# A macaron block with two routed FFNs on one core: closer pacing of GpSimd's transfers, three gather buffers in rotation, and a mix placed by tables

## The chip, the cores and the metric

The kernel runs on one NeuronCore of a Trainium2 chip: TensorE (PE) for matmuls, VectorE (DVE), ScalarE (ACT), GpSimd (POOL) and SyncE (SP, which here only issues DMAs). The metric is the device time of one execution in microseconds; lower is better. Kernels are compared by the median of several runs.

## The reference

x has 8 batches of 512 tokens of 128 channels. Three residual layers follow each other:

```
x = x + 0.5 * moe(layernorm(x))          # 8 experts, top 2 of a softmax, F = 512
x = x + rwkv(layernorm(x))               # token shift, k, v, r, a scan over the sequence, output projection
x = x + 0.5 * moe(layernorm(x))          # the same weights again

moe:  probs = softmax(x @ gate); w, i = top_k(probs, 2); w = w / w.sum()
      out = sum over experts e of  (silu(x @ w1[e]) * (x @ w3[e])) @ w2[e] * w_e
rwkv: k = mix_k(x) @ Wk; v = mix_v(x) @ Wv; r = sigmoid(mix_r(x) @ Wr)
      a running, decayed, numerically shifted sum over the 512 positions of e^k * v and of e^k; r * ratio @ Wo
```

## The kernel before

Tokens are sorted by expert so that TensorE works on tiles of 128 rows that all belong to one expert. There are 177 such tiles. They are grouped in nine *runs* (0 to 8): runs 0 to 3 are the first FFN, each for two batches ("units" .0 and .1), 23 tiles each; runs 4 to 8 are the second FFN. Runs begin at tiles 0, 23, 46, 69, 92, 101, 131, 140 and 162. For each run:

- **Routing** (`NORM`, then `CHOOSE`): layernorm, gate logits, the two picks, counts per expert, and the slot of each token.
- **Scatter** (POOL, L694): for each unit four groups of 128 tokens, twice (top 2), so 8 indirect DMAs a unit, write token rows to their slots in DRAM (`rows_in`). SP then loads the tiles (`rin`), up to six loads ahead.
- **Tiles**: TensorE transposes a tile, multiplies by w1 and w3 (`pa`, `pb`), ACT makes the silu, DVE the product `h` (L1084), TensorE multiplies by w2 three tiles later (`py`), ACT copies `y` out and stores it in DRAM (`rows_out`).
- **Gather** (POOL, L708): 8 indirect DMAs a unit bring the rows of y back to their tokens, in a buffer `yg`. Then DVE's **combine** (L1094) adds them, weighted, to the residual `xres`, eight instructions a unit.
- After a combine of runs 0 to 3 comes the `MIX` chain of that unit (the rwkv layer): DVE, ACT and PE take turns in some twenty steps, from `mstats` to `add`. After a combine of runs 4 to 8 the unit is written to the output.

What is not tile work (routing, combines, mix) is laid between the tiles by a planner, `make_plan`, that runs when the kernel is built. It has a clock with a cost for each step, `ready()` (which steps could start) and `choose()` (the one due first that fits in the slack of a tile). The result is a list: behind tile t, engine by engine, these steps. Every engine runs its list strictly in order, so a step whose input isn't there yet holds all tiles behind it on its engine. The list of POOL's transfers is made by `send()`, which takes `SPACE` us for each.

POOL issues its 256 indirect DMAs in that order. The first 16 follow each other freely. The next 232 are paced, with two rules for each: wait until DVE has made the `h` of tile number `gate`, and wait until the memset behind the transfer before has ended (`s_pace`), then issue, then a small memset (L724). The last 8 (the gather of run 8) are free again. The gather buffer is chosen by unit number (`yg[:, b]`, two of them), so a gather of unit b waits until the last gather of any unit b has been combined. Gathers happen in this order: 0.0, 0.1, 1.0, 1.1, 2.0, 2.1, 3.0, 3.1, 4.0, 4.1, 5.0, 5.1, 6.0, 6.1, 7.0, 8.0.

## Time and profile before

| | us |
|---|---|
| median of 3 runs | 676.24 (674.56 to 677.45) |
| the profiled execution | 672.78 |
| its span, first to last instruction | 671.0 |
| mean granted TensorE clock | 0.946 of full |
| busy: PE, DVE, ACT, POOL | 528.1, 412.7, 319.7, 297.2 |

The profile is of one execution. An instruction's row gives its start, its length, its engine and line, and in brackets how long the engine had been idle before it and what ended that. Tiles can be counted in time by the DVE instruction that makes `h`, one for each tile.

### The profile page before, as it was taken

How to read it: one execution, taken by the hardware profiler on the slowest of the kernel's cores; microseconds unless marked ns; L12 is line 12 of the kernel's file. 1: busy time of each engine (PE TensorE's matmuls, PEld its weight loads, DVE VectorE, ACT ScalarE, POOL GpSimd, SP SyncE). 2: the span in 40 equal slices, each digit the busy share in tenths (PEclk: the TensorE clock that was granted, in tenths of full speed). 3: DMA queues.
4: the chain of work that ended last, by engine and by line, in shares of the span. 5: the costliest groups of instructions: out<-in, count | busy, mean ns of one | idle time of the engine just before them, and what ended most of it. 6: DMA issues, size and time to landing. Idle time of an engine off the chain costs nothing. (4 is left out here: it accounts for less than half of the span.)

```text
span 671.0 us, 18790 instructions
## 1 busy us (share of the span) xinstructions
PE 528.1 (79%) x5866; PEld 482.5 (72%) x5866; DVE 412.7 (62%) x1218; ACT 319.7 (48%) x703; POOL 297.2 (44%) x499
## 2 busy tenths in 40 slices
PE   2136899993899889898999859989789999989500
PEld 1125799893788878677888749878789899879500
DVE  4845975221678789588897848859786443333311
ACT  5433754441484566654656615854645344334100
POOL 1270356666540550565405655046005555525543
PEclk9999999998799999998999959999799999999955
DMA  8943234442221221222211133111112324322311
GB/s 287 325 143 99 84 112 147 136 134 67 76 77 41 64 72 49 73 64 63 78 49 45 53 99 83 44 60 49 57 34 77 100 81 127 85 64 72 86 52 43
DMA packets 89016, 59.57 MB, mean 89 GB/s; under 512 B 10208, under 2 KB 82656, under 8 KB 88928
## 3 DMA queue, kind: packets, MB, share of 16 engines
q1 hardware_dynamic: 55248, 29.97, 15.3%
q0 software_dynamic: 8192, 16.79, 8.9%
q10 hardware_dynamic: 25488, 11.61, 5.9%
q8 instruction: 58, 0.95, 0.6%
q14 instruction: 30, 0.25, 0.1%
HBM read 28.65 MB, written 29.69 MB: 87 GB/s over the span
## 5 line engine op out<-in xcount | busy, mean ns | idle before, releaser
L694 POOL DMA_INDIRECT rows_in<-parts,slot x128 | 132.5, 1035 | 232.9 <-DVE h L1084 136.4
L1084 DVE TENSOR_TENSOR h<-sil,pb 128x512 f32<-128x512 f32 x177 | 120.9, 686 | 145.8 <-PE pb L1201 59.3
L1215 PE MATMUL py<-ffn_w,h 128*128 x1416 | 199.0, 284 | 13.6 <-ACT yrow L753 12.4
L1215 PEld LDWEIGHTS py<-ffn_w,h 128*128 128x128 f32 x1416 | 175.3, 195 | 20.0 <-issue 13.9
L1201 PE MATMUL pa<-rT,ffn_w 128*128 128x128 f16 (+1 forms) x1752 | 152.7, 234 | 36.8 <-DVE h L1084 26.0
L708 POOL DMA_INDIRECT yg<-rows_out,slot x128 | 123.8, 968 | 130.3 <-issue 53.6
L1201 PEld LDWEIGHTS pa<-rT,ffn_w 128*128 x1752 | 124.9, 100 | 52.6 <-issue 41.1
L1201 PE MATMUL pb<-rT,ffn_w 128*128 128x128 f16 (+1 forms) x1752 | 157.1, 233 | 0.1
L1201 PEld LDWEIGHTS pb<-rT,ffn_w 128*128 x1752 | 124.4, 99 | 7.6 <-issue 0.3
L768 ACT ACTIVATE sil<-pa 128x512 f32<-128x512 f32 x177 | 105.4, 595 | 42.6 <-PE pa L1201 32.8
L748 ACT ACTIVATE rT<-pT 128x512 f16<-128x512 f16 (+1 forms) x112 | 56.8, 508 | 92.5 <-PE pT L1188 81.2
L753 ACT ACTIVATE yrow<-py 128x128 f32<-128x128 f32 x177 | 48.6, 274 | 90.0 <-PE py L1215 64.2
L1094 DVE SCALAR_TENSOR_TENSOR xres<-yg,wts,xres 128x128 f32<-128x128 f32 x128 | 36.5, 348 | 63.8 <-DMA yg<-rows_out,slot 63.3
L1188 PE MATMUL pT<-ident,rin 128*128 128x128 f16 x354 | 39.1, 224 | 13.0 <-DMA rin<-rows_in 13.0
L787 ACT ACTIVATE xn<-xres,shift,rstd 128x128 f32<-128x128 f32 x96 | 39.3, 486 | 9.1 <-issue 5.8
L724 POOL MEMSET pace<- 128x64 uint8 x232 | 39.1, 169 | 0.2
L1188 PEld LDWEIGHTS pT<-ident,rin 128*128 128x128 f16 x354 | 26.2, 100 | 14.4 <-DMA rin<-rows_in 13.2
L1268 PE MATMUL bkA<-ident,xn 128*128 128x128 f32 x64 | 12.2, 324 | 29.2 <-ACT xn L787 28.4
L1268 PEld LDWEIGHTS bkA<-ident,xn 128*128 128x128 f32 x64 | 8.8, 170 | 30.0 <-issue 28.8
L1253 PE MATMUL bkB<-xT,qkv_w 128*128 128x512 f16 x96 | 23.4, 379 | 3.4 <-ACT xT L817 3.4
L874 DVE BATCH_NORM_STATS2 stats<-xres 128x6 f32<-128x128 f32 x96 | 20.8, 279 | 4.2 <-DMA xres<-in_x 3.8
L904 DVE TENSOR_TENSOR parts<-xn,parts 128x512 f16<-128x512 f32 x24 | 16.5, 690 | 9.4 <-ACT parts L801 7.7
(155 smaller groups left out, 442.0 us busy)
## 6 DMA issues: line engine op xcount, KB each, us to landing
rows_out<-yrow ACTq DMA_DIRECT2D x177, 64.0 KB
rin<-rows_in SPq DMA_DIRECT2D x65, 128.0 KB
rows_in<-zrow SPq DMA_DIRECT2D x34, 128.0 KB
shared<-in_w SPq DMA_DIRECT2D x16, 256.0 KB, 7.0
rin<-rows_in SPq DMA_DIRECT2D x47, 64.0 KB
rows_in<-zrow SPq DMA_DIRECT2D x2, 1472.0 KB, 12.2
xres<-in_x SPq DMA_DIRECT2D x4, 512.0 KB, 5.7
ffn_w<-in_w SPq DMA_DIRECT2D x8, 256.0 KB
```

The lines of the kernel that those rows point to most:

```text
L694: pool.indirect_dma_start(rows_in[g][:], bass.IndirectOffsetOnAxis(ap=slot[:, c, at:at + 1], axis=0), parts[:, at, :], None).then_inc(s_sc ...
L708: pool.indirect_dma_start(yg[:, b, c, j, :], None, rows_out[SET[run]][0:PASS_STEPS[PASS[run]] * T, :], bass.IndirectOffsetOnAxis(ap=slot[: ...
L724: pool.memset(pace[:], 0).then_inc(s_pace, 1)
L748: act.activation(rT[:, q % 2, :, 0:n], pT[:, :, 0:n], ACT.Copy).then_inc(s_rT, 1)
L753: act.activation(yrow[:, t % YSLOTS, :], py[:], ACT.Copy).then_inc(s_yrow, 1)
L768: act.activation(sil[:, t % 2, :], pa[t % 2][:], ACT.Silu, scale=1.0 / WS).then_inc(s_sil, 1)
L787: ins = act.activation(xn[:, at, j, :], xres[:, js, :][:, j, :], ACT.Identity, bias=shift[:, u, j:j + 1], scale=rstd[:, u, j:j + 1])
L1084: dve.tensor_tensor(h[:, t % RING, :], sil[:, t % 2, :], pb[t % 2][:], ALU.mult).then_inc(s_h, 1)
L1094: ins = dve.scalar_tensor_tensor(xj, yg[:, b, c, j, :], wts[:, c, u * JU + j:u * JU + j + 1], xj, ALU.mult, ALU.add)
L1188: mm = pe.transpose(pT[:, part, n * T:(n + 1) * T], rin[:, q % SLOTS, n, part * D:(part + 1) * D], ident16[:])
L1201: mm = pe.matmul(bank[:, i * cols:(i + 1) * cols], weight_bytes[:, bass.ds(experts[expert_of(t)] * 4 + at, 2 * P)].bitcast(F16), rT[:, q % ...
L1215: mm = pe.matmul(py[:], h[:, step % RING, at:at + T], w, start=(c == 0), stop=(c == FC - 1))
```

## The change

- The pacing memset grows from 64 to 192 bytes a partition and gets four buffers. It now waits for the memset four transfers back, and the DMA itself waits for none. The wait for DVE's tile number is gone: the gate is still in the list, and is not used.
- The gather buffers become three, taken in the order of the gathers, whatever the unit. A gather waits for the combine of the gather three before it. The planner (`in_use`) knows this.
- The last gather (8.0) has a semaphore for each group of 128 tokens (`s_last`). Its combine goes group by group (`combine_last`), and SP writes the output in four parts.
- The planner's costs change a little (`SPACE` 1.6 to 1.5, `LAND` 4.0 to 4.5, others), and two tables are added: `NOT_BEFORE` holds a step back until a tile number, `DUE_SHIFT` makes four chains due later. All 449 steps and 232 paced transfers are the same ones; their order is new.

```diff
+GSLOTS = 3
-PACE = 64
+PACE = 192
+PACES = 4
...
-HOP, LAND, SEND, LOAD = 0.1, 4.0, 1.1, 3.0
-SLIP = {"dve": 6.0, "act": 3.1, "pe": 2.0}
-SPACE = 1.6
+HOP, LAND, SEND, LOAD = 0.1, 4.5, 1.1, 3.0
+SLIP = {"dve": 6.3, "act": 2.9, "pe": 2.0}
+SPACE = 1.5
+DUE_SHIFT = {
+    "stats5.0": 12, "stats2.0": 110, "pick1.0": 173, "combine3.1": 179
+}
+NOT_BEFORE = {
...
+    "place21.0": 8, "hi2.0": 10, "hi3.0": 11, "scatter1.0": 12, "lo2.0": 14, "count2.0": 20, "turn3.1": 20,
...
+        self.due = (due[0] + DUE_SHIFT.get(f'{steps[0]}{run}.{unit}', 0),) + due[1:]
...
-        if any(t is None for t in times):
+        if any(t is None for t in times) or tile < NOT_BEFORE.get(f'{step}{c.run}.{c.unit}', EARLY):
...
+    def in_use(run, unit):
+
+        order = [p[2:] for p in plan if p[1] == "gather"]
+        n = order.index((run, unit))
+        return n >= GSLOTS and "combine" not in gathered[order[n - GSLOTS]].ends
...
-        yg = sb("yg", [P, UG, TOPK, JU, D])
+        yg = sb("yg", [P, GSLOTS, TOPK, JU, D])
...
+                    if (run, b) == GATHERS[-1]:
+                        for j in range(JU):
+                            sp.wait_ge(s_lastc, j + 1)
+                            sp.dma_start(ov[:, js, :][:, j, :], xres[:, js, :][:, j, :]).then_inc(s_out, 16)
+                        return
...
-                if (j, c) == (0, 0):
-                    before = [p[1:] for p in PLAN if p[1] == "gather" and p[3] == b]
-                    at_b = before.index(("gather", run, b))
-                    if at_b:
-                        pool.wait_ge(s_comb, count(("combine",), ("combine", before[at_b - 1][1], b)))
+                n = GATHERS.index((run, b))
+                if (j, c) == (0, 0) and n >= GSLOTS:
+                    pool.wait_ge(s_comb, count(("combine",), ("combine", *GATHERS[n - GSLOTS])))
...
-            for sent, (gate, name, *one) in enumerate(TRANSFERS):
-                wait(pool, s_h, gate)
-                wait(pool, s_pace, sent)
+            for sent, (_, name, *one) in enumerate(TRANSFERS):
                 if name == "scatter":
                     scatter(*one)
                 else:
                     gather(*one)
-                pool.memset(pace[:], 0).then_inc(s_pace, 1)
+                wait(pool, s_pace, sent - PACES + 1)
+                pool.memset(pace[:, sent % PACES, :], 0).then_inc(s_pace, 1)
...
+            def combine_last(run, b):
+
+                u, js = units(run, b)
+                slot_ = (len(GATHERS) - 1) % GSLOTS
+                for j in range(JU):
+                    xj = xres[:, js, :][:, j, :]
+                    dve.wait_ge(s_last[j], 16 * TOPK)
+                    for c in range(TOPK):
+                        ins = dve.scalar_tensor_tensor(xj, yg[:, slot_, c, j, :],
+                                                       wts[:, c, u * JU + j:u * JU + j + 1], xj, ALU.mult, ALU.add)
+                        if c == 0:
+                            link(ins)
+                    ins.then_inc(s_lastc, 1)
```

Two places show how the rows move. The first is on POOL, where its first gather (unit 0.0) begins. `rows_in2` and `rows_in3` are written by scatters of runs 2 and 3, `yg` by gathers. Before:

```order
L694 DMA rows_in3<-parts,slot 2944x256 [waits transfer_spaced,h_made]
L724 MEMSET pace 128x64
L708 DMA yg<-rows_out0,slot 128x128 [waits y_stored4,y_stored5,y_stored3,y_stored6,y_stored2,y_stored7,y_stored1,y_stored8,y_stored0,y_stored9,transfer_spaced,h_made]
L724 MEMSET pace 128x64
L708 DMA yg<-rows_out0,slot 128x128 [waits transfer_spaced,h_made]
```

And after:

```order
L727 DMA rows_in2<-parts,slot 2944x256
L755 MEMSET pace 128x192 [waits transfer_spaced]
L739 DMA yg<-rows_out0,slot 128x128 [waits y_stored5,y_stored6,y_stored4,y_stored7,y_stored3,y_stored8,y_stored2,y_stored9,y_stored1,y_stored0]
L755 MEMSET pace 128x192 [waits transfer_spaced]
L739 DMA yg<-rows_out0,slot 128x128
```

Before, 39 paced transfers stand ahead of this gather (runs 1 and 2 complete, and 7 of run 3). After, 26 do: run 1 and ten of run 2; the other six of run 2 and all of run 3 stand behind the gathers of 0.0 and 0.1. The combine of 0.0 stands behind 35 `h` on DVE before, and behind 37 after.

The second place is the end of DVE's list: the combines of 7.0 and of 8.0. Before, both use buffer 0:

```order
L1094 SCALAR_TENSOR_TENSOR xres<-yg,wts,xres 128x128 [waits gathered1]
L1094 SCALAR_TENSOR_TENSOR xres<-yg,wts,xres 128x128 x3
L1094 SCALAR_TENSOR_TENSOR xres<-yg,wts,xres 128x128 [waits dve_chain]
L1094 SCALAR_TENSOR_TENSOR xres<-yg,wts,xres 128x128 x3
L1094 SCALAR_TENSOR_TENSOR xres<-yg,wts,xres 128x128 [waits gathered0,combined]
```

And after:

```order
L1125 SCALAR_TENSOR_TENSOR xres<-yg,wts,xres 128x128 [waits gathered2,combined]
L1125 SCALAR_TENSOR_TENSOR xres<-yg,wts,xres 128x128 x3
L1125 SCALAR_TENSOR_TENSOR xres<-yg,wts,xres 128x128 [waits dve_chain]
L1125 SCALAR_TENSOR_TENSOR xres<-yg,wts,xres 128x128 x3
L1140 SCALAR_TENSOR_TENSOR xres<-yg,wts,xres 128x128 [waits last_gathered0,combined]
L1140 SCALAR_TENSOR_TENSOR xres<-yg,wts,xres 128x128 [waits dve_chain]
L1140 SCALAR_TENSOR_TENSOR xres<-yg,wts,xres 128x128 [waits last_gathered1]
```

Unit 7.0 has moved to buffer 2, and of the last unit only two instructions now stand behind the last group's arrival.

## Rows read from the trace of the kernel before

**Rows 1.** The page: granted TensorE clock in 40 slices, and two groups.

```profile
PEclk9999999998799999998999959999799999999955
...
L708 POOL DMA_INDIRECT yg<-rows_out,slot x128 | 123.8, 968 | 130.3 <-issue 53.6
...
L724 POOL MEMSET pace<- 128x64 uint8 x232 | 39.1, 169 | 0.2
```

**Rows 2.** Instructions on `h` by stretch: PE, PEld, DVE busy (DVE's count is tiles).

```profile
57.50:151.50 94.00, 34.22 (x254) 30.77 (x255) 23.33 (x34) 1.00 0.39 115
151.50:240.70 89.20, 26.78 (x192) 23.92 (x191) 15.60 (x23) 0.92 0.23 64
240.70:400.50 159.80, 49.21 (x346) 43.47 (x344) 30.14 (x44) 0.95 0.23 65
400.50:501.70 101.20, 34.22 (x241) 29.77 (x240) 20.54 (x30) 0.97 0.19 54
501.70:599.00 97.30, 38.55 (x278) 33.59 (x279) 23.01 (x34) 1.00 0.32 90
```

**Rows 3.** What DVE waited for, gathers only: whole span, 150:240, 600:627, 627:671.

```profile
DVE xres L1094 <- DMA yg<-rows_out,slot: 63.3, 14, 13.1
...
DVE xres L1094 <- DMA yg<-rows_out,slot: 18.0, 3, 13.1
...
DVE xres L1094 <- DMA yg<-rows_out,slot: 0.3, 1, 0.3
...
DVE xres L1094 <- DMA yg<-rows_out,slot: 32.1, 3, 12.7
```

**Rows 4.** Timeline of DVE: the combine of unit 0.0.

```profile
165.39 2.32 DVE L1094 SCALAR_TENSOR_TENSOR xres<-yg,wts,xres 128x128 f32<-128x128 f32 x8 [13.12 <-DMA yg<-rows_out,slot]
```

**Rows 5.** Timeline of PE after that wait.

```profile
169.98 1.46 PE L1201 MATMUL pa<-rT,ffn_w 128*128 128x128 f16 x12 [13.49 <-DVE h L1084]
```

**Rows 6.** Busy by engine (PE, PEld, DVE, ACT, POOL), then granted clock.

```profile
169.00:175.10 6.10, 5.12 (x40) 5.06 (x41) 4.11 (x15) 3.10 (x8) 3.83 (x8) 0.51 0.21 58
```

**Rows 7.** Timeline of POOL: a scatter of run 3, and the first gather.

```profile
136.41 0.97 POOL L694 DMA_INDIRECT rows_in<-parts,slot  x1 [0.75 <-issue]
...
149.67 0.99 POOL L708 DMA_INDIRECT yg<-rows_out,slot  x1 [0.79 <-DVE h L1084]
```

**Rows 8.** Timeline of PE at the start of run 5.

```profile
388.65 0.61 PE L1188 MATMUL pT<-ident,rin 128*128 128x128 f16 x4 [4.08 <-DMA rin<-rows_in]
...
397.60 1.46 PE L1201 MATMUL pa<-rT,ffn_w 128*128 128x128 f16 x12 [5.25 <-issue]
```

**Rows 9.** Timeline of POOL in the tail, units 6.0 to 8.0.

```profile
601.76 0.95 POOL L708 DMA_INDIRECT yg<-rows_out,slot  x1 [9.90 <-DVE h L1084]
...
646.06 0.95 POOL L708 DMA_INDIRECT yg<-rows_out,slot  x1 [0.75 <-POOL pace L724]
...
651.79 0.95 POOL L708 DMA_INDIRECT yg<-rows_out,slot  x1 [4.61 <-DVE xres L1094]
653.05 0.95 POOL L708 DMA_INDIRECT yg<-rows_out,slot  x1 [0.30 <-issue]
...
660.55 0.94 POOL L708 DMA_INDIRECT yg<-rows_out,slot  x1 [0.30 <-issue]
```

**Rows 10.** Timeline from 661 to the end: the last combine and write.

```profile
663.28 2.31 DVE L1094 SCALAR_TENSOR_TENSOR xres<-yg,wts,xres 128x128 f32<-128x128 f32 x8 [12.26 <-DMA yg<-rows_out,slot]
665.68 0.37 SPq L651 DMA_DIRECT2D out<-xres  x1
```

**Rows 11.** Timeline of ACT: the last y copied out and stored.

```profile
631.65 0.28 ACT L753 ACTIVATE yrow<-py 128x128 f32<-128x128 f32 x1 [1.29 <-issue]
```

**Rows 12.** Timeline of POOL: a memset at the start, a scatter at 35 us.

```profile
0.73 0.20 POOL L671 MEMSET ident<- 128x128 f32 x1 [0.29 <-POOLq L1344]
...
35.38 1.96 POOL L694 DMA_INDIRECT rows_in<-parts,slot  x1 [0.30 <-issue]
```

**Rows 13.** Busy by engine (PE, PEld, DVE, ACT, POOL) in two stretches.

```profile
400.50:501.70 101.20, 91.97 (x1149) 85.60 (x1148) 83.30 (x242) 58.19 (x124) 29.99 (x52) 0.97 0.19 54
501.70:599.00 97.30, 90.52 (x1144) 86.53 (x1145) 42.80 (x125) 40.80 (x94) 53.07 (x94) 1.00 0.32 90
```

More of the change, by code:

```diff
@@ L157, in __init__ @@
     def __init__(self, steps, run, unit, due, start, follows=()):
-        self.steps, self.run, self.unit, self.due, self.start = steps, run, unit, due, start
+        self.steps, self.run, self.unit, self.start = steps, run, unit, start
+        self.due = (due[0] + DUE_SHIFT.get(f'{steps[0]}{run}.{unit}', 0),) + due[1:]
         self.follows, self.ends = list(follows), {}
@@ L187, in tile @@
         q, half, _ = TILE_OF[t]
-        up1 = max(self.free["pe"], self.rT[q] + HOP, self.h.get(t - 2, 0.0) + HOP) + UP
+        up = UP if paired(t) else UP_ALONE
+        up1 = max(self.free["pe"], self.rT[q] + HOP, self.h.get(t - 2, 0.0) + HOP) + up
         if t > SKEW:
@@ L191, in tile @@
         turned = self.turn(q + 1, up1) if t + 1 < TILES and TILE_OF[t + 1][1] == 0 else up1
[L192 removed]
+        up3 = turned + up
         silu = max(self.free["act"], up1 + HOP) + SILU
@@ L311, in ask @@
         waiting.append([due, at, name, run, [(b, j, c) for b in units for j in range(JU) for c in range(TOPK)]])
+    def in_use(run, unit):
+        order = [p[2:] for p in plan if p[1] == "gather"]
+        n = order.index((run, unit))
+        return n >= GSLOTS and "combine" not in gathered[order[n - GSLOTS]].ends
     def send(tile, until):
         while True:
-            now = [w for w in waiting if w[1] <= until and not (w[2] == "gather" and any(
-                c.next() == "combine" for c in chains if c.unit == w[4][0][0] and gathered.get((c.run, c.unit)) is c
-                and c.run < w[3]))]
+            now = [w for w in waiting if w[1] <= until and not (w[2] == "gather" and in_use(w[3], w[4][0][0]))]
             at = max([free["pool"]] + [min((w[1] for w in now), default=until)])
@@ L385, in count @@
     return order.index(upto) + 1
+GATHERS = [p[2:] for p in PLAN if p[1] == "gather"]
 def run_of(t):
@@ L445, in macaron_kernel @@
         zrow = sb("zrow", [P, 2 * D], F16)
-        pace = sb("pace", [P, PACE], U8)
+        pace = sb("pace", [P, PACES, PACE], U8)
         e_desc = sb("e_desc", [P, JG, E])
@@ L558, in macaron_kernel @@
         s_yst = [sem(f"y_stored{i}") for i in range(YSLOTS)]
-        s_gat = [sem(f"gathered{b}") for b in range(UG)]
+        s_gat = [sem(f"gathered{i}") for i in range(GSLOTS)]
+        s_last = [sem(f"last_gathered{j}") for j in range(JU)]
+        s_lastc = sem("last_combined")
         s_comb = sem("combined")
@@ L665, in _ @@
             last_steps(step)
-            sp.wait_ge(s_out, 16 * B)
+            sp.wait_ge(s_out, 16 * (B - 1 + JU))
         @block.gpsimd
@@ L702, in gather @@
                         pool.wait_ge(s_yst[k], 16 * len(range(k, PEND[run], YSLOTS)))
[L703 to L707 removed]
+                n = GATHERS.index((run, b))
+                if (j, c) == (0, 0) and n >= GSLOTS:
+                    pool.wait_ge(s_comb, count(("combine",), ("combine", *GATHERS[n - GSLOTS])))
                 pool.indirect_dma_start(
[L709 to L710 removed]
+                    yg[:, n % GSLOTS, c, j, :], None, rows_out[SET[run]][0:PASS_STEPS[PASS[run]] * T, :],
+                    bass.IndirectOffsetOnAxis(ap=slot[:, c, at:at + 1], axis=0)).then_inc(
+                        s_last[j] if n + 1 == len(GATHERS) else s_gat[n % GSLOTS], 16)
             def every(run, units):
@@ L1088, in combine @@
                 u, js = units(run, b)
-                runs = [p[2] for p in PLAN if p[1] == "gather" and p[3] == b]
-                dve.wait_ge(s_gat[b], 16 * TOPK * JU * (runs.index(run) + 1))
+                n = GATHERS.index((run, b))
+                dve.wait_ge(s_gat[n % GSLOTS], 16 * TOPK * JU * (n // GSLOTS + 1))
                 for c in range(TOPK):
@@ L1106, in step @@
                 if name == "combine":
-                    combine(run, b)
+                    (combine_last if (run, b) == GATHERS[-1] else combine)(run, b)
                 if name in ("stats", "mstats"):
```

10 lines of the change are left out of this document (4 added, 6 removed), and 7 rows, old and new, of the table NOT_BEFORE.

## The prediction

> **What bounds the kernel now.** I read the page first, for the slices in which the clock or PE's digit falls; then the instructions on `h` by stretch, since one of DVE's is one tile; then what DVE and PE waited for; and last the timelines of POOL, DVE and PE at the longest of those waits. The reader is to see three things.
>
> First, in most stretches the tiles go at a steady pace that all three compute engines set together: 44 tiles in 159.8 us (3.63 each), 30 in 101.2 (3.37), 34 in 97.3 (2.86) [rows 2]. PE is busy 92.0 of 101.2 us there, DVE 83.3 [rows 13]. Nothing in the change makes this work smaller, so the gain must come from waits.
>
> Second, one stretch is slow without more work: 23 tiles in 89.2 us, 3.88 each, at a mean clock of 0.92 [rows 2]. DVE stands 13.12 us before the combine of unit 0.0, because the gather has not landed [rows 4], and PE stands 13.49 us behind it, since every `h` queues behind that combine [rows 5].
>
> Third, the last 45 us hold no tiles at all. POOL is still issuing gathers at its spacing, 601.76 to 646.06 for 24 of them, then pauses, and issues eight more [rows 9]. The chain ends there. DVE waited 63.3 us for gathers in 14 waits over the span, of which 32.1 are three waits in the tail and 0.3 one just before it [rows 3]. That leaves 30.9 us in ten waits in mid-kernel: the 13.1 one, and nine that share 17.8.
>
> **The new spacing.** This decides most terms. Between paced transfers before: (149.67 - 136.41) / 7 = 1.89 us [rows 7], which is 0.97 of DMA instruction, 0.17 of memset and 0.76 until the next one, a wait on the memset's semaphore. Without pacing the gap is 0.30 and the step 1.25 [rows 9]. After the change no DMA waits for a memset, so I take the 0.30. The memset is three times as long in elements. A memset of 128 elements a partition took 0.20 us [rows 12] against 0.17 for 64 [rows 1]; that is 0.03 for 64 more, hence 0.23 or 0.24 for 192. Sum: 0.95 + 0.24 + 0.30 = 1.49. Lower end: 1.25, if the memset runs inside the gap. Upper end: a memset three times as long (0.51) and the full 0.75 again, 2.21. I take 1.49, since the row without a wait on the DMA is the nearest.
>
> **Term 1, the tail.** (a) The 23 steps from 601.76 to 646.06 took 1.93 each; at 1.49 they save 23 x 0.44 = 10.0. (b) The gather of 8.0 waited for the combine of 7.0, which had its buffer: 651.79 - 646.06 = 5.73 [rows 9]. With three buffers it waits for the combine of 6.0, long done, and follows after 1.49: 4.2 saved. (c) Behind the last landing stand two instructions instead of eight: 2.31 becomes 0.6 [rows 10], 1.7 saved. The write behind them and the end, 671.0 - 665.7 = 5.3, stay. Together 15.9. What is late next: the last y, copied at 631.65 [rows 11]. The gather of 8.0 would start at 601.76 + 24 x 1.49 = 637.5, after it, so all of it counts; at 1.25 it would be 631.8, and some 3 us of the further gain would be lost to this wait. Ends: 5.5 (spacing stays as it was) to 19. DVE still does 8 instructions for 6.1 and for 7.0, under POOL's transfers.
>
> **Term 2, the first gather.** Seven scatters of run 3 stood before it, between 136.41 and 149.67. Its inputs, the y of tile 22, were made some four tiles behind tile 22, at about 134 to 136 (34 tiles in 94 us, 2.8 each [rows 2]). Now it can start at 136. Eight transfers at 1.49 put the last start at 146.4, and it lands 2.7 later as at the end (663.28 - 660.55 [rows 9, 10]): 149. Its combine has moved two tiles back, to about 155. So the 13.1 goes whole. The second unit's last start is 136 + 15 x 1.49 = 158.4, landed 161, for a combine near 163: also no wait. The clock goes with it: after PE's 13.5 us of idleness the granted clock stood at 0.51 of full, the 1.2 GHz level, from 169.0 to 175.1, with PE busy 5.1 of 6.1 us [rows 6]; half of that, 3, comes back. Term 2 is 16. Ends: 8 (another wait appears in its place) to 19.
>
> **Term 3, the nine other waits in mid-kernel**, 17.8 us [rows 3]. Each block of 16 transfers gets 16 x 0.4 = 6 us shorter and no longer waits for tile numbers, so most fall below zero, but a tile whose DVE was early may then wait for PE or ACT. I count half, 9. Ends: 0 and 18.
>
> **Term 4, the start of run 5**: 4.08 us on a load of `rin`, then 5.25 of "issue" [rows 8]. The scatters of run 5 are nearer to their deadline than any others. They start two tiles later now (3.4 x 2 = 7 us) and take 6 us less, so the load wait hardly moves; the second part may or may not recur. I count 3. Ends: 0 and 12.
>
> **Term 5, what the tables cost.** The second half of the mix of unit 3.1 moves from before tile 131 to behind it, six tiles at the pace of 3.37 instead of 2.86: 3 us lost. Cover is there, DVE being busy 42.8 of 97.3 us behind tile 131 [rows 13]. In the first 34 tiles the same routing work is spread over more tiles; I count nothing, ends 4 lost and 6 gained.
>
> The third buffer, the semaphores and the four writes (64 KB each, three of them under the gather) cost nothing: they lie on SP and in memory.
>
> Sum: 15.9 + 16 + 9 + 3 - 3 = 41. Span 671.0 - 41 = 630. The execution's own time is 1.8 above its span (672.78): 631.8. The median shown is 3.5 above that execution, so 635 as a median.
>
> **A rule against it.** One scatter took 1.96 us instead of 0.96 [rows 12]; 123.8 us over 128 gathers, 968 ns on average, says that this is rare [rows 1]. The Trainium skill (SBUF — State Buffer, "Who interferes with whom") states that GpSimd and a two-port VectorE instruction lock each other out whole. By that rule a denser stream of transfers meets more such instructions in the same time. The trace agrees that it happens, but each transfer meets as many as before, so it makes a rival and no term.
>
> **Rivals.**
> - *The spacing does not fall (about 1.9).* For it: the step is set by POOL's own dispatch, and 0.76 is what the trace shows beside a memset; against it, the 0.30 without one. Then term 1 is 5.5, term 2 still 13 or so (136 + 7 x 1.9 + 2.7 = 152), terms 3 and 4 nothing, and combines placed for a faster stream wait: 3 us lost at each of three pairs. 671 - 5.5 - 13 + 3 + 9 = 664; with the 5.3 on top, 669 or so. 7 in 100.
> - *Slower than before: the spacing grows to 2.2*, the memset running its full length under the same semaphore gap. A block of 16 takes 35 us where the placement allows for 24. The combine of the second unit then comes 11 us late at each of seven pairs of gathers, less some 3 of slack: 56 lost, PE's idleness bringing the half clock beside it. 671 - 18 + 56 = 709, as a median 714. It decides from a spacing of about 2.05 on. 3 in 100.
> - *The waits move.* The transfers are in time, but steps held back by the table end up against the starts of runs, and term 3 comes to nothing, term 4 too, with 5 to 8 us lost behind tile 131. 671 - 32 + 12 = 651, median 656. For it: PE is busy above 90% there, so there is little room to catch up in. 13 in 100.
> - *Locked-out transfers*, by the port rule: two of 16 transfers of each of 14 blocks take 1 us more, some half of it seen. 14 us on the stream, 5 on the time: 640. 7 in 100.
>
> **Numbers.** The forecast has 70 in 100. The range, 619 to 656, takes in spacings down to 1.25 (3 more from the tail), terms 3 and 4 at their upper ends (18 more would be 614; I cut at 619), and up to the third rival. The measurement tells changes of 0.5%, 3.4 us, from none. Faster 0.95, same 0.02 (a mixture of the first and third rival), slower 0.03.
>
> **What would show it.** The timeline of POOL: steps of 1.49 between paced transfers, and no 0.75 gaps (term 1a; 1.9 would be the first rival, 2.2 the second). DVE's waits for gathers: 63.3 falls under 25, most of it in the tail, with none of 13 (terms 2 and 3). The granted clock has no half-speed stretch near 165 us. The last gather follows the one before without a pause, and from the end of the tiles to the end of the span are some 28 to 30 us instead of 45. The number of tiles by stretch: tile 57 before 222 us instead of 240.7. It is wrong if PE's pace from tile 57 on is worse than 3.6 us a tile, or if a new wait over 8 us stands in mid-kernel.

## The result, and the profile after

| | before | after |
|---|---|---|
| median, us | 676.85 (674.56 to 677.63, 4 runs) | 809.52 (799.02 to 820.80, 4 runs) |
| the profiled execution | 672.78 | 811.93 |
| its span | 671.0 | 810.1 |
| mean granted clock | 0.946 | 0.859 |

The ratio is 1.187 [1.176, 1.199]: slower by a fifth, where I had forecast 635 us. It is taken from the two fast runs of after alone, 799.0 and 807.1 us; the profiled one is one of the two slow ones. The second half of the result came only with the last experiment. The same kernel, byte for byte, took 614.9 us in a later sitting, beside a kernel before of 672.7 there: 0.913 [0.910, 0.916]. The chip of every experiment was noted, and it differs between sittings. That of the result above was not, nor that of the trace of before. I call it chip 1, or the first chip, and the later one the other chip, though all that is known is that the sitting was another. So there are two questions below: what makes the kernel slow on the first chip, and whether the working of the prediction holds on the other.

First the page of after, with the lines that answer to [rows 1]: the clock by slice, DVE's combines, the gathers and the paced memset (busy us, mean ns, idle time before).

```profile
PEclk9999889859699899989988699997985698697595
...
L739 POOL DMA_INDIRECT yg<-rows_out,slot x128 | 124.9, 976 | 159.9 <-issue 107.4
...
L755 POOL MEMSET pace<- 128x192 uint8 x232 | 64.0, 276 | 0.2
...
L1125 DVE SCALAR_TENSOR_TENSOR xres<-yg,wts,xres 128x128 f32<-128x128 f32 x120 | 34.2, 347 | 0.6
```

The transfers did what I had said. Each is as long as before (976 ns, 968 in [rows 1]), the memset went from 169 to 276 ns, and DVE's combines of all units but the last were kept waiting 0.6 us; those of the last waited 12.8, which makes 13.4 in place of the 63.3 of [rows 3]. POOL's timeline has the step, to be set against [rows 7]:

```profile
416.58 0.27 POOL L755 MEMSET pace<- 128x192 uint8 x1
417.01 0.96 POOL L727 DMA_INDIRECT rows_in<-parts,slot  x1 [0.17 <-issue]
417.98 0.27 POOL L755 MEMSET pace<- 128x192 uint8 x1
418.42 0.96 POOL L727 DMA_INDIRECT rows_in<-parts,slot  x1 [0.17 <-issue]
```

The step is 0.96 + 0.27 + 0.17 = 1.40 us; I had said 1.49. Now what the engines waited for in after, longest first (total us, times, longest):

```profile
POOL rows_in L727 <- DVE slot L1040: 299.3, 9, 71.2
ACT yrow L784 <- remote: 127.1, 29, 10.8
DVE h L1115 <- remote: 110.1, 17, 16.4
...
ACT yrow L784 <- PE py L1260: 66.2, 76, 2.3
```

"Remote" stands where the update of the awaited semaphore is recorded just before the instruction, but every instruction that could have made it had ended at least 1.5 us earlier. The kernel runs on one core and no wait of before had that name. The timeline of the stretch 736 to 748, under a block of 16 gathers, shows what such a wait is (start, length, instruction, idle time before it):

```profile
736.15 1.16 PE L1260 MATMUL py<-ffn_w,h 128*128 x8 [1.09 <-ACT yrow L784]
...
739.08 0.59 ACT L799 ACTIVATE sil<-pa 128x512 f32<-128x512 f32 x1
...
740.77 0.47 PE L1246 MATMUL pb<-rT,ffn_w 128*128 128x128 f16 x2
741.69 0.38 PE L1246 MATMUL pb<-rT,ffn_w 128*128 128x128 f16 x2 [0.45 <-issue]
743.10 0.48 PE L1246 MATMUL pb<-rT,ffn_w 128*128 128x128 f16 x3 [1.03 <-issue]
744.53 0.58 PE L1246 MATMUL pb<-rT,ffn_w 128*128 128x128 f16 x4 [0.95 <-issue]
...
744.75 0.69 DVE L1115 TENSOR_TENSOR h<-sil,pb 128x512 f32<-128x512 f32 x1 [5.80 <-remote]
...
747.46 0.28 ACT L784 ACTIVATE yrow<-py 128x128 f32<-128x128 f32 x1 [7.79 <-remote]
```

Two things are to be seen. ACT copies at 747.46 a `py` whose last matmul was over at 737.31, though ACT has been idle since 739.67: what the matmul's end should have released came 7.8 us late or more. And one group of twelve matmuls, which wait for nothing between them, is torn: two, two, three, four, and one more at 745.96, with 0.45 to 1.03 us of "issue" between, the later pieces 1.41 and 1.43 us apart, as the transfers are. POOL's transfers and DVE's own chains go on at their usual pace beside it. The whole execution has 65 gaps over 0.25 us between two matmuls of one tile of which the second waits for nothing, 38.4 us together; before had none. (One expectation below speaks of 97 torn groups; by this rule there are 65.)

The trace also records the updates of the semaphores, and they say whose hand-overs are late. All 78 waits of after on "remote" are for an update that TensorE makes. For the `py` above it is recorded at 747.44, 10.1 us behind the matmul's end, and ACT starts 0.02 us later. Count as late an update 0.3 to 15 us behind the end of the last instruction that makes it: of TensorE's 724, 156 are late, 122 of them by over 1.5 us; of ACT's 526, none; of DVE's, one, as in the run on the other chip too. So it is not hand-overs at large that are late, but TensorE's. Whether the update alone was held back or the matmul's result with it the trace cannot tell, because the ends of matmuls are modelled.

The trace of before has the same thing on a small scale. 45 of TensorE's 627 recorded updates are late there, by 0.3 to 0.8 us, and each of them comes 1.3 to 1.5 us behind the start of a transfer of POOL. One of them, an update for `pT` recorded at 182.92:

```profile
181.64 1.06 POOL L694 DMA_INDIRECT rows_in<-parts,slot  x1 [0.78 <-issue]
...
182.04 0.28 PE L1188 MATMUL pT<-ident,rin 128*128 128x128 f16 x2
...
182.94 0.39 ACT L748 ACTIVATE rT<-pT 128x256 f16<-128x256 f16 x1 [0.61 <-PE pT L1188]
```

The matmuls are over at 182.32, ACT is idle, and starts 0.62 us later. With 1.89 us between transfers there is time for this before the next one starts; with 1.40 us the next one has started or is about to. That this is why the small delay grows into queues of up to 10 us is my reading of the rows, and no run tests it.

TensorE's matmuls are the same 5866. They were busy 587.0 us of 810.1 in after, 519.4 of 613.6 in the run on the other chip: of the 196.5 us between the two, 128.9 are idleness and 67.6 are longer matmuls. The mean clock, 0.859 against 0.976, accounts for about that much (519.4 x 0.976 / 0.859 = 590). From 600 to 640 the granted clock stood at 0.53, the 1.2 GHz level, with PE busy 16.5 of 40 us.

And the same kernel on the other chip. The page, then POOL's timeline in the tail:

```profile
PEclk9999999999999999999999989999999999989985
...
L755 POOL MEMSET pace<- 128x192 uint8 x232 | 64.5, 278 | 0.2
...
L1125 DVE SCALAR_TENSOR_TENSOR xres<-yg,wts,xres 128x128 f32<-128x128 f32 x120 | 34.2, 347 | 5.6 <-DMA yg<-rows_out,slot 5.0
```

```profile
558.45 0.95 POOL L739 DMA_INDIRECT yg<-rows_out,slot  x1 [21.32 <-DMA rows_out<-yrow]
559.84 0.95 POOL L739 DMA_INDIRECT yg<-rows_out,slot  x1 [0.17 <-issue]
...
590.58 0.95 POOL L739 DMA_INDIRECT yg<-rows_out,slot  x1 [0.17 <-issue]
...
594.47 0.95 POOL L739 DMA_INDIRECT yg<-rows_out,slot  x1 [2.67 <-issue]
...
603.23 0.94 POOL L739 DMA_INDIRECT yg<-rows_out,slot  x1 [0.30 <-issue]
```

Twenty-four gathers at (590.58 - 558.45) / 23 = 1.40 us: the same step as on the first chip. But the clock is at 0.8 of full or more in all slices but the last, and there is no torn group, no "remote" and no late update of TensorE's. The packets of POOL's transfers took the same time in both, 115 ns on average, so it is not slower transfers that part the two runs. The waits of ACT for the same copy, and the pair of rows that answers to the late one above:

```profile
ACT yrow L784 <- PE py L1260: 86.0, 104, 2.3
```

```profile
563.26 1.11 PE L1260 MATMUL py<-ffn_w,h 128*128 x8
...
564.40 0.28 ACT L784 ACTIVATE yrow<-py 128x128 f32<-128x128 f32 x1 [0.74 <-PE py L1260]
```

### The profile page after: what moved, and what is told of

Read it like the earlier page. It is cut to its first block, busy times and chain, and to the rows that moved or that the text cites. A ratio compares the mean times of both kernels' runs of the same rounds, so it can differ in the third digit from the quotient of the medians.

```text
span 810.1 us, 18562 instructions
## 1 busy us (share of the span) xinstructions
PE 587.0 (72%) x5866; PEld 513.8 (63%) x5866; DVE 414.6 (51%) x1218; ACT 319.1 (39%) x703; POOL 318.7 (39%) x499
## 3 DMA queue, kind: packets, MB, share of 16 engines
q1 hardware_dynamic: 55296, 29.97, 12.7%
## 4 chain that ended last, share of the span: by engine, by line
PE 49%; another core or an unknown queue 22%; issue 12%; ACT 9%; SPq 4%; DVE 3%; DMA 1%; POOL 1%; POOLq 0%; ACTq 0%; DVEq 0%
PE py L1260 17%; PE pa L1246 12%; PE pb L1246 10%; PE bkB L1298 3%; PE pT L1233 2%; ACT sil L799 2%; ACT rT L779 1%; ACT xn L818 1%; ACT yrow L784 1%; PE bkA L1298 1%; PE bkB L1319 1%; SPq L653 1%; PE bkA L1313 1%; SPq L640 1%
## 5 line engine op out<-in xcount | busy, mean ns | idle before, releaser
L1260 PE MATMUL py<-ffn_w,h 128*128 x1416 | 218.4, 301 | 70.4 <-ACT yrow L784 52.5
L727 POOL DMA_INDIRECT rows_in<-parts,slot x128 | 128.6, 1005 | 321.1 <-DVE slot L1040 299.3
L1260 PEld LDWEIGHTS py<-ffn_w,h 128*128 128x128 f32 x1416 | 190.6, 209 | 85.6 <-issue 58.2
L1246 PE MATMUL pa<-rT,ffn_w 128*128 128x128 f16 (+1 forms) x1752 | 165.3, 244 | 52.1 <-issue 40.0
L1246 PE MATMUL pb<-rT,ffn_w 128*128 128x128 f16 (+1 forms) x1752 | 174.6, 242 | 32.1 <-issue 31.5
L1246 PEld LDWEIGHTS pa<-rT,ffn_w 128*128 x1752 | 131.7, 104 | 75.2 <-issue 63.1
L1246 PEld LDWEIGHTS pb<-rT,ffn_w 128*128 x1752 | 130.1, 103 | 50.1 <-issue 42.7
L784 ACT ACTIVATE yrow<-py 128x128 f32<-128x128 f32 x177 | 48.5, 274 | 197.8 <-remote 127.1
L755 POOL MEMSET pace<- 128x192 uint8 x232 | 64.0, 276 | 0.2
L1233 PE MATMUL pT<-ident,rin 128*128 128x128 f16 x354 | 41.3, 230 | 10.8 <-DMA rin<-rows_in 8.9
L818 ACT ACTIVATE xn<-xres,shift,rstd 128x128 f32<-128x128 f32 x96 | 39.2, 485 | 10.3 <-DVE shift L927 8.0
L1298 PE MATMUL bkB<-xT,qkv_w 128*128 128x512 f16 x96 | 26.3, 411 | 0.7 <-issue 0.5
L905 DVE BATCH_NORM_STATS2 stats<-xres 128x6 f32<-128x128 f32 x96 | 20.9, 280 | 4.3 <-DMA xres<-in_x 3.9
L1319 PEld LDWEIGHTS bkB<-gate_w,xnT 128*128 128x128 f32 x128 | 18.9, 226 | 3.2 <-issue 2.3
```

What stands on the lines that cost most here:

```text
L727: pool.indirect_dma_start(rows_in[g][:], bass.IndirectOffsetOnAxis(ap=slot[:, c, at:at + 1], axis=0), parts[:, at, :], None).then_inc(s_sc ...
L755: pool.memset(pace[:, sent % PACES, :], 0).then_inc(s_pace, 1)
L784: act.activation(yrow[:, t % YSLOTS, :], py[:], ACT.Copy).then_inc(s_yrow, 1)
L818: ins = act.activation(xn[:, at, j, :], xres[:, js, :][:, j, :], ACT.Identity, bias=shift[:, u, j:j + 1], scale=rstd[:, u, j:j + 1])
L1233: mm = pe.transpose(pT[:, part, n * T:(n + 1) * T], rin[:, q % SLOTS, n, part * D:(part + 1) * D], ident16[:])
L1246: mm = pe.matmul(bank[:, i * cols:(i + 1) * cols], weight_bytes[:, bass.ds(experts[expert_of(t)] * 4 + at, 2 * P)].bitcast(F16), rT[:, q % ...
```

## The experiments

The runs fell in five sittings, and only before the last did I take in that the chip changes between them. So each is given with its chip: chip 1 is that of the result above, 2 to 5 those of the experiments in their order (two sittings fell on chip 3). "Torn" counts the gaps inside groups of matmuls, "late" the late updates of TensorE's and, in brackets, those by over 1.5 us, both by the rules above; "remote" is the row of the waits for ACT's copy of `py`. "DMA events" is the share of the semaphore updates of DMAs that the trace has, of the 16 that each transfer makes.

| run | chip | step, us | torn: gaps, us | late | DMA events | remote: us, times | median, us | ratio to before |
|---|---|---|---|---|---|---|---|---|
| before | 1 | 1.89 | none | 45 (0) | 60% | none | 676.9 |  |
| after | 1 | 1.40 | 65, 38.4 | 156 (122) | 60% | 127.1, 29 | 809.5 | 1.187 [1.176, 1.199] |
| a1_old_pace | 2 | 1.41 | 50, 32.0 | 150 (119) | 60% | 109.7, 26 | 815.5 | 1.211 [1.200, 1.221] |
| b2_no_gates | 2 | 1.41 | 54, 31.0 | 150 (123) | 61% | 101.2, 27 | 818.3 | 1.215 [1.195, 1.235] |
| b1_new_pace | 2 | 1.41 | 17, 7.0 | 197 (101) | 62% | 35.6, 13 | 707.3 | 1.050 [1.043, 1.058] |
| a2_long_memset | 2 | 1.89 | none | 59 (0) | 55% | none | 646.0 | 0.959 [0.955, 0.963] |
| a3_pace320 | 3 | 1.51 | none | none | 97% | none | 618.2 | 0.916 [0.911, 0.921] |
| a3_pace448 | 3 | 1.62 | none | none | 96% | none | 623.1 | 0.923 [0.917, 0.929] |
| m1_five_memsets | 3 | 1.64 | none | none | 96% | none | 625.2 | 0.926 [0.921, 0.932] |
| c1_fixed_expert | 3 | 1.41 | none | none | 98% | none | 593.3 | 0.879 [0.873, 0.885] |
| a5_pace256 | 3 | 1.46 | none | none | 97% | none | 618.4 | 0.918 [0.915, 0.920] |
| d1_before_320 | 3 | 1.51 | none | none | 98% | none | 634.7 | 0.941 [0.939, 0.943] |
| c2_fixed_320 | 3 | 1.51 | none | none | 98% | none | 599.6 | 0.889 [0.887, 0.892] |
| a6_no_tables | 3 | 1.51 | none | none | 97% | none | 624.4 | 0.927 [0.924, 0.929] |
| e1_up_fixed | 4 | 1.40 | none | none | 98% | none | 602.7 | 0.895 [0.893, 0.896] |
| e2_down_fixed | 4 | 1.40 | none | none | 97% | none | 607.7 | 0.903 [0.901, 0.904] |
| e3_half_gathers | 4 | 1.40 | none | none | 97% | none | 614.9 | 0.912 [0.910, 0.914] |
| e4_pace224 | 4 | 1.43 | none | none | 97% | none | 615.8 | 0.915 [0.913, 0.917] |
| f1_after_again | 5 | 1.40 | none | none | 97% | none | 614.9 | 0.913 [0.910, 0.916] |
| f2_down_fixed_again | 5 | 1.40 | none | none | 98% | none | 610.0 | 0.906 [0.902, 0.909] |

**First sitting: the spacing or the missing waits for tiles?** The rate theory says that it is the dense stream of transfers that starves TensorE; the gate theory says that it is transfers going out at tiles at which before held them back. Four runs on chip 2. The old pacing in the changed kernel (memset of 64 bytes, the wait for it ahead of the DMA):

```diff
-PACE = 192
+PACE = 64
+                wait(pool, s_pace, sent)
                 if name == "scatter":
 ...
-                wait(pool, s_pace, sent - PACES + 1)
```

> The changed kernel with the pacing of before: memset of 64 bytes a partition, and each DMA waits for the memset of the transfer before, so steps of 1.87 to 1.9 us; tables, buffers, the last unit and the missing tile gates stay new. Theory R (the dense stream of transfers, steps of 1.4 us, starves PE): 640 to 665 us, and no 12-matmul group of PE torn apart. Rival P (the new placement is at fault, whatever the spacing): 780 to 820 us.

It came to 815.5 us, because its premise fell: the step was 1.41, not 1.87. With one wait on the DMA in place of two (the gate's and the memset's) the gap ahead of it was 0.28 us and not 0.75. So it is no test of the old spacing, but it shows that it takes both waits to make the spacing of before. The waits for tiles taken from the kernel before has the same surprise:

```diff
-                wait(pool, s_h, gate)
                 wait(pool, s_pace, sent)
```

> The kernel before without the waits for DVE's tile number ahead of each transfer, spacing as before (1.87 us). Theory R: within 1.5% of before (665 to 685), since the step stays 1.87. Rival G (the gates kept transfers away from PE's busy stretches, and their loss is the cause): over 720 us.

Again the step fell to 1.41, and the order of before took 818.3 us. The gate theory's number was hit, but by way of the spacing. The new pacing in the kernel before, gates kept:

```diff
-PACE = 64
+PACE = 192
+PACES = 4
 ...
-                wait(pool, s_pace, sent)
 ...
+                wait(pool, s_pace, sent - PACES + 1)
+                pool.memset(pace[:, sent % PACES, :], 0).then_inc(s_pace, 1)
```

> The kernel before with the new pacing alone (192 bytes, four buffers, the wait on the memset and not on the DMA); order, tile gates and gather buffers are those of before. Theory R: 720 to 820 us, with torn matmul groups under the blocks of transfers, though tile gates slow some blocks and so spare some of it. Rival P: 660 to 680 us, some us faster for the tail.

At 1.41 us, broken up by the gates, it took 707.3, a little under the 720 to 820 of the rate theory and far over the 660 to 680 of its rival. And the changed kernel with a long memset:

```diff
-PACE = 192
+PACE = 768
```

> The changed kernel with a pacing memset of 768 bytes instead of 192; no DMA waits for a memset. By the two lengths seen (0.169 us for 64, 0.276 for 192) it takes 0.76 us, which makes steps of about 1.89 us with POOL never waiting. Theory R (the rate of transfers): 640 to 665 us, as with the old pacing. Rival W (PE starves because POOL runs without a wait for a semaphore between its DMAs, whatever the rate): over 760 us.

646.0 us without one gate: the gates are not needed. The rows of these four on one chip are the test of the rate theory. This is "remote" for ACT's copy in a1, b2 and b1, in that order; a2 has no such row.

```profile
ACT yrow L784 <- remote: 109.7, 26, 10.2
```

```profile
ACT yrow L752 <- remote: 101.2, 27, 7.3
```

```profile
ACT yrow L754 <- remote: 35.6, 13, 6.0
```

The page's row of a2 for the memset, whose 755 ns is the whole difference to after:

```profile
L755 POOL MEMSET pace<- 128x768 uint8 x232 | 175.1, 755 | 0.2
```

On chip 2 the loss comes with the spacing, in two orders of work, and is gone at 1.89. What is left there, in a2 as in before, are late updates of under 0.8 us, 59 of them.

**Second sitting: where is the edge, and what is starved?** Memsets of 320 and of 448 bytes, and five short ones in place of one long one, to part the time between transfers from the number of POOL's instructions:

```diff
-PACE = 192
+PACE = 320      (a3_pace320; 448 in a3_pace448)
```

> The changed kernel with a pacing memset of 320 bytes: by 0.83 ns a byte (0.166 us for 64, 0.753 for 768) 0.38 us, a step of 1.50 us. Theory R (a rate of transfers above which PE starves) says only that it lies between: near 810 if the limit is slower than 1.50, near 640 if it is between 1.40 and 1.50. I expect 640 to 700 us, since blocks of the changed kernel that ran at 1.48 us tore few groups. Rival W (POOL without a wait in its queue): refuted already by 646 us at 1.885.

> The changed kernel with a pacing memset of 448 bytes, a step of 1.61 us. Theory R with a limit near 1.5: 630 to 642 us, below the 646 of a step of 1.885, since the tail's 23 steps take 0.27 us less each (6 us). With a limit at 1.7 or so: over 660 us.

```diff
-                pool.memset(pace[:, sent % PACES, :], 0).then_inc(s_pace, 1)
+                for i in range(5):
+                    pool.memset(pace[:, sent % PACES * 5 + i, :], 0).then_inc(s_pace, 1)
```

> The changed kernel with five memsets of 64 bytes behind each transfer instead of one of 192: some 0.17 us each, so steps near 1.9 us again, with six instructions of POOL in each instead of two. Theory R (the indirect DMAs are what starves PE): 640 to 660 us. Rival I (the number of POOL instructions with semaphore counts in a time starves it): over 760 us.

And all tiles with expert 0's weights at fixed addresses, which leaves the choice of the expert out and with it the register additions that stand between TensorE's matmuls (2,774 in the trace of the changed kernel, some 16 a tile):

```diff
-            weight_bytes[:, bass.ds(experts[expert_of(t)] * 4 + at, 2 * P)]
+            weight_bytes[:, at:at + 2 * P]
```

> The changed kernel, step 1.40 us, with the weights of expert 0 for every tile: PE's matmuls have fixed addresses, and its 2,774 register instructions are gone. The choice of expert by tile is left out of the computation. Theory R as it stands (any PE instruction stream starves): 780 to 820 us. Rival A (it is the matmuls with register addresses that starve): 615 to 660 us.

618.2, 623.1, 625.2 and 593.3 us. All four lie below what was expected of them, and the five memsets made a step of 1.64 us and not 1.9, so they part time from number less well than meant. I read them as: the edge lies between 1.40 and 1.51 us of step, and additions from registers are what is starved. Neither reading had a ground, since they compared chip 3 with chips 1 and 2.

**Third sitting, chip 3.** A step nearer to the edge; the order of before with the new pacing and no gates; the fixed addresses at the wider step; and the changed kernel with both tables empty.

```diff
-PACE = 192
+PACE = 256      (a5_pace256; 320 in the other three)
-                wait(pool, s_h, gate)          (d1_before_320)
-DUE_SHIFT = { ... }
-NOT_BEFORE = { ... }
+DUE_SHIFT = {}
+NOT_BEFORE = {}                                (a6_no_tables)
```

> The changed kernel with memsets of 256 bytes a partition instead of 192: a step of POOL of about 1.45 us, halfway between the 1.40 at which it took 809.5 us and the 1.51 at which it took 618.2. Rate theory with an edge (PE's matmuls are torn apart only from some rate of transfers on, then each other one more): either side of the edge, so at most 640 us with fewer than 20 torn groups, or at least 760 with over 60; rate theory without an edge (each 0.01 us of step counts): about 700 to 730 us. Either way TensorE's groups of twelve tell which.

> The kernel before, order of work and tables as they were, without the wait for a tile ahead of each transfer and with the paced transfers of the best run (four buffers, memsets of 320 bytes): step 1.51 us, where the same order took 818 us at 1.41. Rate theory: no torn groups, so faster than the 676 before; by the differences between runs (1.885 to 1.51 us of step was worth 27.8 us in the changed order) about 648 us. If instead the order of before needs its waits for tiles, whatever the rate: over 680 us.

> The changed kernel with memsets of 320 bytes, and every tile working with expert 0's weights at fixed addresses (the choice of the expert is left out), as in the run with a step of 1.40 us that took 593.3 us. Theory: addresses from registers have a price of their own, dense transfers or not; then this one stays near 593 to 600 us, and some 20 of the 216 us that fixed addresses gained there were this price. Rival: fixed addresses only spare the torn groups; then it takes the 618 us of the same step with registers, or a little over it.

> The changed kernel with memsets of 320 bytes and both tables empty (no first tiles, no shifted due times): the planner's own order, with the new spacing, the three gather buffers and the last unit by blocks. Theory: the tables bring the mix's steps to where tiles wait least and carry 5 to 15 us, so 623 to 633 us against 618.2; rival: spacing and buffers carry it all, 615 to 621; other rival: the order of the planner alone starts the runs late, over 640.

These four and the 618.2 of a3 share a chip, and what they say of each other stands: 618.4, 634.7 (I had said about 648), 599.6 and 624.4. From the before of that sitting (674.0) to d1 is 39.3 us: the spacing and the missing gates. From d1 to a6, 10.3: three buffers, last unit by blocks, the planner's new costs. From a6 to a3, 6.2: the tables. Fixed addresses are worth 18.6 us (618.2 to 599.6) with nothing starved, so that price is real; c1 had led me to put over 200 on it.

**Fourth sitting, chip 4.** A part of the additions (e1 is without 2,336 of the 2,774, e2 without 584), and gathers of half the bytes:

```diff
-    weight_bytes[:, bass.ds(experts[expert_of(t)] * 4 + at, 2 * P)]      (e1_up_fixed)
+    weight_bytes[:, at:at + 2 * P]
-    weight_bytes[:, bass.ds(experts[expert_of(t)] * 4 + 4 * (UPW + c * D), 4 * D)]
+    weight_bytes[:, 4 * (UPW + c * D):4 * (UPW + c * D) + 4 * D]         (e2_down_fixed)
-                    yg[:, n % GSLOTS, c, j, :], None, rows_out[...],
+                    yg[:, n % GSLOTS, c, j, 0:D // 2], None,
+                    rows_out[...].rearrange("r (h c) -> (r h) c", h=2),   (e3_half_gathers)
-PACE = 192
+PACE = 224                                     (e4_pace224)
```

> The changed kernel at its own step of 1.40 us, the up-projections (pa, pb) with expert 0's weights at fixed addresses, the down-projection (py) still with addresses from registers (the expert's choice is left out of the up-projections alone): of TensorE's additions between matmuls some 16 of 20 a tile are gone. Theory: it is these additions in its stream that dense transfers starve, in proportion to their number; then no torn groups and about 600 us. Rival: any address from a register is enough, and a tile's few still cost; then torn groups stay and it takes over 700 us.

> The mirror of it: the down-projection with expert 0's weights at fixed addresses, the up-projections with registers, step 1.40 us. Theory: the torn groups are those of pa and pb, whose additions stay; so over 60 torn groups and 770 to 800 us. Rival (the sum of all additions counts, and the edge is near): fewer than 40 torn groups and under 700 us.

> The changed kernel at its step of 1.40 us, with gathers that fetch half of each row (256 bytes instead of 512, the first half of a row's place in a table of half rows; the other half of the gathered rows is left out), the same number of transfers and of their parts. If the bytes moved starve TensorE, the 50 torn groups of 97 that fell under gathers go and about 720 us are left; if the number of transfers and of their parts does it, 790 to 820 us.

> The changed kernel with memsets of 224 bytes: a step of about 1.43 us, between the 1.40 that took 809.5 us and the 1.46 that took 618.4. An edge between two neighbouring values lies on one side of it: within 10 us of 618 or above 760; a steep slope gives 650 to 750.

All four were fast: 602.7, 607.7, 614.9, 615.8. Removing any of three unlike things (additions, bytes, 0.03 us of step) seemed to cure it, and halving the gathers seemed to cure also the groups torn under scatters. It is unlikely that causes so unlike all sit at one edge. What the four had in common with c1 and not with after was the later sitting, on another chip.

**Fifth sitting, chip 5.** The changed kernel itself, and one of its fast relatives, together.

> The changed kernel again, unchanged. All runs at steps near 1.40 us that were slow (809.5, and 815.5, 818.3 and 707.3 with its relatives) ran in the first two of five sittings, all that were fast at such steps (593.3 to 615.8) in later ones, on other chips. If the cause lies in the kernel (transfers of every byte, additions between the matmuls, step of 1.40), it takes 800 to 820 us here too, and the later comparisons stand; if the chip decides, it can take about 612 to 616 us here, what a step of 1.43 took.

> The run with the down-projection's weights at fixed addresses (expert 0's for all tiles; the expert's choice is left out there), again, on the same chip as the changed kernel. It took 607.7 us. If the additions removed were what cured it, again 605 to 611 us beside a changed kernel at over 800; if the chip decides, both are fast within 10 us of one another, or both slow.

614.9 and 610.0. The same kernel is slow in one sitting and fast in another, so the kernel alone does not decide.

**What is shown, and what stays open.** Shown: on chip 2 steps of 1.41 us make TensorE's hand-overs late and tear its groups, in two orders of work, and a step of 1.89 does not cost that time; after has the same picture at 1.40 on chip 1. On chips 3 to 5 there is nothing of it, at steps down to 1.40. The kernel before, whose step is 1.89, takes 673 to 677 us on all five, so nothing in its times tells them apart. The traces do. The six earliest, put down here to chips 1 and 2 and with before and a2 among them, all have late updates of TensorE's, and of the updates of DMAs they hold 55 to 62%; the 14 of chips 3 to 5 have no late update and hold 96 to 98%. So the difference is there at the old spacing too, and the dense stream makes it cost time.

Open is what differs. It may be the chips, but chips 1 and 2 ran first and the others later, no chip ran in both groups, and the hour or what else the machine was doing would fit as well. Since every execution here was traced, and events are missing from the traces in just these sittings, an effect of the tracing itself is not excluded either. Open too: where between 1.41 and 1.89 the edge lies on chip 2; whether chips 1 and 2 are one and the same; and whether fewer additions or fewer bytes would help on such a chip, since e1 to e3 never ran on one. Instruction fetches are not it, as far as the trace shows: 58 of 16 KB in both profiles of the changed kernel, each starting at the same place in TensorE's stream to within 53 instructions, where two fetches are some 256 apart.

## Why the prediction was wrong, step by step

**The step that failed on the first chip** is the one under the first point: "Nothing in the change makes this work smaller, so the gain must come from waits". I took the tiles' pace of 2.9 to 3.6 us as given by the three engines and out of reach of POOL's stream. It was not: the 34 tiles from 131 on took 141.8 us, 97.3 before, and the 11 from 165 on took 53.4, 26.9 before, at clocks of 0.80 and 0.71. From tile 57 to the last the pace was 4.2 us a tile, which is the sign of being wrong that the text had set at 3.6. What the runs showed in place of this step: TensorE's updates and groups of matmuls are held up under POOL's transfers (156 late updates, 65 torn gaps), and TensorE stood idle 128.9 us longer and ran 67.6 us longer than in the sitting where they are not. Why it is held up stays open. The rows are those on `h` by stretch, to be set against [rows 2] (a tile on a border counts in both stretches):

```profile
57.60:192.10 134.50, 39.62 (x256) 34.86 (x256) 23.11 (x35) 0.85 0.30 85
192.10:285.70 93.60, 27.26 (x180) 24.12 (x181) 15.79 (x24) 0.89 0.20 57
285.70:475.00 189.30, 54.03 (x352) 46.97 (x351) 30.12 (x45) 0.89 0.20 56
475.00:586.90 111.90, 36.59 (x245) 31.66 (x245) 20.39 (x30) 0.92 0.15 44
586.90:728.70 141.80, 42.79 (x276) 37.41 (x275) 23.38 (x35) 0.80 0.21 58
728.70:782.10 53.40, 13.82 (x86) 11.99 (x85) 7.61 (x12) 0.71 0.24 64
```

No rival had it. The one that spoke of a denser stream let it cost the transfers, by the port rule, 5 us; here the transfers lost nothing (976 ns on average), TensorE did, and with it those that wait for it. The rule weighed there (the Trainium skill, "SBUF — State Buffer", "Who interferes with whom") locks GpSimd and VectorE against each other; no run here shows that at work in the loss, since POOL's transfers and DVE's own chains kept their pace. For the slow scatter of [rows 12], which I took as agreement, the trace says only that it ran beside a DVE instruction with two inputs (L1052). The rival on the other side needed a step of 2.2 us, and got the sign for a reason that did not occur. I also gave 0.95 to "faster" on one trace of one chip, in which a spacing under 1.89 in mid-kernel does not occur: the rows had nothing on what a denser stream does to the other engines, and that should have been a bound of its own, with both signs. The trace of before held the sign, 45 late updates of TensorE's behind transfers, but no figure for what they become at 1.40 us, and nothing to say that another sitting would be without them.

**On the other chip the steps can be checked one by one.** The stretches of that run:

```profile
57.60:146.60 89.00, 34.17 (x254) 30.87 (x255) 23.01 (x34) 1.00 0.42 120
146.60:214.90 68.30, 25.32 (x188) 22.55 (x186) 15.71 (x24) 1.00 0.31 85
214.90:362.00 147.10, 47.91 (x347) 42.16 (x346) 29.97 (x45) 0.99 0.25 72
362.00:460.80 98.80, 34.01 (x243) 29.54 (x243) 20.40 (x30) 1.00 0.19 53
460.80:557.10 96.30, 39.92 (x278) 35.06 (x278) 23.30 (x35) 0.96 0.31 86
557.10:585.30 28.20, 11.63 (x86) 10.10 (x85) 7.44 (x12) 1.00 0.40 107
```

Against [rows 2] and the same tiles of before (26.9 us for the sixth stretch, 45.1 behind it) the gain is 5.0 + 20.9 + 12.7 + 2.4 + 1.0 - 1.3 + 16.8 = 57.5 of span; forecast were 41.

- *Spacing*: 1.40 for 1.49. The memset was 0.04 us longer than I took it; the gap was 0.17, and not the 0.30 that I had read where DMAs follow one another [rows 9].
- *Term 1, tail, 15.9*: 45.1 us became 28.3, a gain of 16.8; "28 to 30" was asked for, and after has 28.0 even on the first chip. The pause before the last eight gathers is 2.67 us instead of 4.61 [rows 9], and by the times the last `y`, copied at 591.1, ends it, which the text had said only of a step near 1.25. The last combines of the run (idle before in brackets), for [rows 10]:

```profile
603.24 0.74 DVE L1140 SCALAR_TENSOR_TENSOR xres<-yg,wts,xres 128x128 f32<-128x128 f32 x2 [1.67 <-DMA yg<-rows_out,slot]
...
605.76 0.74 DVE L1140 SCALAR_TENSOR_TENSOR xres<-yg,wts,xres 128x128 f32<-128x128 f32 x2 [1.78 <-DMA yg<-rows_out,slot]
```

- *Term 2, first gather, 16*: the combine of unit 0.0 stands at 151.53 with no wait, and the clock is full there. The second stretch gained 20.9, in which some of term 3 is.

```profile
129.78 0.98 POOL L739 DMA_INDIRECT yg<-rows_out,slot  x1 [0.25 <-issue]
```

```profile
151.53 2.36 DVE L1125 SCALAR_TENSOR_TENSOR xres<-yg,wts,xres 128x128 f32<-128x128 f32 x8
```

- *Term 3, nine other waits, 9 of 17.8*: I had halved it for tiles that would wait for another engine instead. DVE's waits for gathers came to 13.0 us, all of them behind 585 (under 25 was asked for), so the whole 17.8 went in mid-kernel. The half kept back is at most 9 of the 16.5 us missing from my sum, and the 5.0 of the first 34 tiles are the next part, which by a6 is the tables' work.
- *Term 4, run 5, 3*: the wait of 4.08 us for `rin` is gone and the 5.25 of "issue" is 4.91 [rows 8]. A gain of 4.4.

```profile
359.16 1.46 PE L1246 MATMUL pa<-rT,ffn_w 128*128 128x128 f16 x12 [4.91 <-issue]
```

- *Term 5, the tables, -3*: the wrong sign. Emptying them cost 6.2 us (a6 against a3, both on chip 3). The tables gained 5.1 us in the first 34 tiles, 94.1 us against 89.0, where I had counted nothing with 6 as the upper end, and 5.9 in the next 23, which I had not looked at. Behind tile 131 they do cost, 92.6 and 26.5 us becoming 96.5 and 28.2: 5.6, and I had said 3.

So the mechanism was right on this chip, with term 3 sized too low and term 5 of the wrong sign, and 614.9 us lies 4 below the range. In the sitting of the result the forecast was wrong in sign.

## What to carry to other kernels

When a change makes a stream of GpSimd transfers denser, treat "the other engines don't notice" as a claim with a price, and look in the profile for hand-overs from TensorE that come late ("remote" or "issue" before instructions whose inputs have long been there) and for groups of matmuls torn at the transfers' beat. Look for small ones in the kernel before, too. Pace such a stream no denser than the gain needs: here the widest step, 1.89 us with the new order, was 0.959 of before on a chip where 1.41 was 1.21 of it, while on a chip without the trouble 1.51 and 1.46 were alike (618.2 and 618.4). And before a surprise is explained, run the same kernel again beside its variants: eight of the runs here (the second and fourth sittings) looked for causes that one repetition would have put in doubt.

## What the runs showed of the hardware

- In some sittings dense indirect transfers (in blocks of 16, one every 1.40 us) go with late semaphore updates of TensorE's, so that ACT waited up to 10.8 us for a finished tile: on chip 2, 26 and 27 waits on "remote" for ACT's copy at 1.41 us and none at 1.89; on chips 3 to 5 none at 1.40 to 1.64. At 1.41 with the stream broken up by waits for tiles there were 13. Updates of ACT's own were not late in any run.
- In the same sittings TensorE's updates are late at 1.89 us too (45 in before, 59 in a2), by at most 0.8 us, and each is recorded 1.3 to 1.5 us behind the start of a transfer.
- The gap before a transfer depends on what it waits for: 0.17 us with no wait (after) or with a wait for a tile alone (b1), 0.28 with a wait for the memset just ahead of it (a1, b2), 0.76 with both (before). Taking the wait for the tile away made the spacing a quarter shorter (1.89 to 1.41) and, on chip 2, the kernel a fifth slower (b2).
- GpSimd's memset took 167, 277, 385 and 755 ns for 64, 192, 320 and 768 bytes a partition: about 0.83 ns a byte above 114 ns. It paces a queue finely.
- Register instructions between matmuls cost 18.6 us of 618 here: a3 has 2,920 of them in TensorE's stream and c2 none, so some 6 ns each.
